# Layer totals of a graph network: one product and a VectorE transpose instead of four products and an ACT copy, at other places of the step

## What is computed

```python
z = jnp.einsum('nc,kco->nko', x, W)                       # 64 taps of 32 x 32
msg = jnp.zeros((src.shape[0], W.shape[2]), x.dtype)
for s in range(basis.shape[1]):                           # 8 corners of a cell
    msg = msg + basis[:, s, None] * z[src, wi[:, s]]
agg = jax.ops.segment_sum(msg, dst, num_segments=n)       # sum over a node's edges
agg = agg / jnp.clip(cnt, 1.0)[:, None]
return agg + x @ R + b
```

## Time and profile before

| | us |
|---|---|
| runs, median of 3 | 20890.9 (20882.26 to 20961.26) |
| profiled execution, its own time | 20959.69 |
| span of the profiled execution | 20957.9 |
| first part, until the first step of the first layer | 6021.5 |
| a layer's 98 steps | about 4790 to 4820, three times |

### The profile page before, as it was taken

One profiled execution on the slowest core, in us unless ns is written; L12 is line 12 of the kernel. 1 busy time (PEld: TensorE's weight loads), 2 busy tenths in 40 slices (PEclk: granted clock), 3 DMA queues, 4 the chain that ended last, 5 costly groups with the idle time before them and its releaser, 6 DMA issues.

```text
span 20957.9 us, 179979 instructions
## 1 busy us (share of the span) xinstructions
PE 15299.0 (73%) x55111; PEld 8212.8 (39%) x55111; DVE 11387.0 (54%) x19145; ACT 3304.1 (16%) x4009; POOL 11380.3 (54%) x12003
## 2 busy tenths in 40 slices
PE   7788888888866767676666676667666676766676
PEld 3333333333333444443433343444443343434343
DVE  4556666656655555555545555555555555555555
ACT  1111111111111111111111111111111111111111
POOL 5445555555545555555545555555554555555554
PEclk7666666666678888888878888888887888888888
DMA  1000000000010000000010000000001000000000
GB/s 33 13 14 15 15 15 15 15 14 15 15 24 16 16 16 16 16 16 16 16 23 16 17 16 16 16 16 16 17 16 23 16 16 16 16 16 16 16 16 22
DMA packets 886190, 353.06 MB, mean 17 GB/s; under 512 B 604191, under 2 KB 877680, under 8 KB 885872
## 3 DMA queue, kind: packets, MB, share of 16 engines
q0 software_dynamic: 386208, 210.78, 5.9%
q1 hardware_dynamic: 329276, 112.29, 2.3%
q10 hardware_dynamic: 170644, 29.29, 0.8%
HBM read 314.88 MB, written 36.56 MB: 17 GB/s over the span
## 4 chain that ended last, share of the span: by engine, by line
PE 51%; another core or an unknown queue 28%; issue 14%; ACT 3%; DVE 3%; ACTq 1%; DMA 0%; POOL 0%; DVEq 0%; SPq 0%; POOLq 0%
PE ps L1547 17%; PE ps L1559 16%; PE ps L1459 5%; PE ps L1570 4%; PE ps L1475 3%; ACT big L792 2%; PE ps L1448 2%; PE ps L1442 2%; DVE big L1056 1%; PE ps L1432 1%; ACT big L710 1%; ACTq L802 1%; ACT big L700 0%; PE ps L1414 0%
## 5 line engine op out<-in xcount | busy, mean ns | idle before, releaser
L571 POOL DMA_INDIRECT xg<-x_rows,idx x8790 | 8316.4, 946 | 6310.6 <-DVE big L1254 3682.7
L1547 PE MATMUL ps<-big 128*128 128x256 f32 x18816 | 5050.5, 422 | 1286.7 <-ACT big L792 1250.4
L1237 DVE TENSOR_TENSOR big<-ps,onehot 128x1024 f32<-128x1024 f32 x2352 | 2864.7, 1218 | 5084.9 <-remote 3417.8
L1547 PEld LDWEIGHTS ps<-big 128*128 128x128 f32 x18816 | 3863.2, 211 | 3111.9 <-issue 2581.3
L571 POOL DMA_INDIRECT xg<-in_x,idx x3125 | 2974.6, 952 | 2806.5 <-DVE big L1026 1826.0
L1570 PE MATMUL ps<-big,w_taps 128*32 128x512 f32 x9408 | 1544.9, 734 | 3060.8 <-issue 2851.8
L792 ACT COPY big<-ps 128x1024 f32<-128x1024 f32 x2352 | 2353.5, 1013 | 8828.4 <-PE ps L1547 5318.7
L1559 PE MATMUL ps<-xw,big 128*128 128x512 f32 x8232 | 3671.5, 597 | 50.5 <-issue 23.2
L1459 PE MATMUL ps<-w,big 65*128 65x256 f32 x6272 | 2498.1, 541 | 126.9 <-DVE big L1056 85.6
L1559 PEld LDWEIGHTS ps<-xw,big 128*128 128x128 f32 x8232 | 1543.4, 190 | 2006.9 <-issue 1981.1
L1459 PEld LDWEIGHTS ps<-w,big 65*128 65x128 f32 x6272 | 1566.0, 267 | 1875.0 <-issue 1562.7
(11 more groups left out here) (139 smaller groups left out, 6620.8 us busy)
## 6 DMA issues: line engine op xcount, KB each, us to landing
xg<-x_rows,idx POOLq DMA_INDIRECT x8790
xg<-in_x,idx POOLq DMA_INDIRECT x3125
row_of<-pick_rows SPq DMA_DIRECT2D x294, 128.0 KB
agg_rows<-rts ACTq DMA_DIRECT2D x294, 64.0 KB
meta<-in_coord_t SPq DMA_DIRECT2D x294, 48.0 KB
big<-in_rad SPq DMA_DIRECT2D x196, 64.0 KB
meta<-meta_items SPq DMA_DIRECT2D x392, 32.0 KB
idx<-in_src_t SPq DMA_DIRECT2D x392, 16.0 KB
```

Of the source, the lines that this page charges most:

```text
L571: return nc.gpsimd.indirect_dma_start(out=dst_tile, out_offset=None, in_=table, in_offset=bass.IndirectOffsetOnAxis(ap=index, axis=0))
L1237: v.tensor_tensor(bm[:, ring], hat_outer[:, its].rearrange("p n c b -> p n (c b)").unsqueeze(3) .to_broadcast([P, 4, 16, J]), onehot[:, it ...
L1547: tr = nc.tensor.matmul(ps[:, 2 * (ch % 2) + r // 2, 256 * (r % 2):256 * (r % 2) + 256], xm[:, at].rearrange("p a c -> p (a c)"), bm[:, at ...
```

## The change

Totals: one product with `fold` as the weights (32 columns) and all 512 columns of `R` moving, in place of four products with `R` as weights. It leaves 32 x 512 totals in bank 7, not turned. DVE turns them (32 x 32 blocks) straight out of PSUM into `rts` (`turn_layer`) and signals `rt_out`; ACT copies nothing any more and stores 32 rows of 2 KB instead of 512 pieces of 128 bytes. Places: the scan stands behind chunk 3 instead of 2 on DVE; the totals behind chunk 4 instead of 3 on PE; the turn behind chunk 6 on DVE; the store ahead of chunk 7 instead of 4 on ACT; tap products 0 and 1 behind chunk 6, 2 and 3 behind chunk 7, instead of one behind each of chunks 4 to 7.

```diff
-        rts = sb("rts", [P, ROW0])
+        rts = sb("rts", [2 * CH, ROW0])
             def l1_step(l, i, par, with_rows):
                 for ch in range(8):
-                    if ch == 4 and with_rows:
+                    if ch == 7 and with_rows:
                         l1_rows(l, i - 2)
             def l1_rows(l, i):
-                act.wait_ge(rt_ready, l * STEPS + i + 1)
-                act.wait_ge(rows_stored, rows0(path) + 16 * (l * STEPS + i))
-                nc.scalar.copy(rts[:, 0:P], ps[:, 7, 0:P]).then_inc(rt_out, 1)
                 act.wait_ge(rt_out, (l + 1) * STEPS + i + 1)
-                to = agg_rows[ds(i * STEP, STEP), :].rearrange("i (q s f) -> s i q f", q=4, s=4)
-                act.dma_start(to, rts[:, 0:P].rearrange("p (q f) -> p q f", q=4)).then_inc(rows_stored, 16)
+                act.dma_start(agg_rows[ds(i * STEP, STEP), :], rts[0:CH, 0:ROW]).then_inc(rows_stored, 16)
+            def turn_layer(l, i):
+
+                dve.wait_ge(rt_ready, l * STEPS + i + 1)
+                dve.wait_ge(rows_stored, rows0(path) + 16 * (l * STEPS + i))
+                v.transpose(rts[0:CH, 0:ROW], ps[0:CH, 7, :]).then_inc(rt_out, 1)
-                    if ch == 2 and with_scan:
+                    if ch == 3 and with_scan:
                         scan(n - 2, prior + LINKS1, P, l + 1, par, twice - 2)
+                    if ch == 6 and with_scan:
+                        turn_layer(l, i - 2)
                 for i in (STEPS - 2, STEPS - 1):
                     scan((l + 1) * STEPS + i, steps[0], P, l + 1, i % 2, 2 * (i // 2 + 1))
                     steps[0] += SCAN
+                    turn_layer(l, i)
             def totals_by_cell(n):
                 pe.wait_ge(R_ready, n + 1)
-                for q in range(4):
-                    tr = nc.tensor.matmul(ps[:, 7, CH * q:CH * q + CH],
-                                          R[:, 4 * q:4 * q + 4, :].rearrange("p s i -> p (s i)"), fold[:],
-                                          start=True, stop=True)
-                tr.then_inc(rt_ready, 1)
+                nc.tensor.matmul(ps[0:CH, 7, :], fold[:], R[:].rearrange("p s i -> p (s i)"), start=True, stop=True,
+                                 tile_position=(0, 0)).then_inc(rt_ready, 1)
-                    if with_totals and ch == 3:
+                    if with_totals and ch == 4:
                         totals_by_cell((l + 1) * STEPS + i - 2)
-                    if with_taps and ch >= 4:
-                        tap_products(l, i - 1, 1 - par, ch - 4)
+                    if with_taps and ch >= 6:
+                        for t in (2 * ch - 12, 2 * ch - 11):
+                            tap_products(l, i - 1, 1 - par, t)
```

More of the change, by code:

```diff
@@ L976, in turn_first @@
                     dve.wait_ge(rows_stored, 32 * n)
-                v.transpose(rts[0:2 * CH, 0:ROW], R[0:2 * CH].rearrange("p s i -> p (s i)")).then_inc(rt_out, 1)
+                v.transpose(rts[:, 0:ROW], R[0:2 * CH].rearrange("p s i -> p (s i)")).then_inc(rt_out, 1)
+            def turn_layer(l, i):
+                dve.wait_ge(rt_ready, l * STEPS + i + 1)
+                dve.wait_ge(rows_stored, rows0(path) + 16 * (l * STEPS + i))
+                v.transpose(rts[0:CH, 0:ROW], ps[0:CH, 7, :]).then_inc(rt_out, 1)
             base0 = steps[0]
```

## The result

| | before | after |
|---|---|---|
| median of the runs, us | 20906.85 (20882.26 to 20961.26, 4 runs) | 21165.83 (21105.84 to 21216.51, 4 runs) |
| span of the profiled execution, us | 20957.9 | 21146.0 |
| a step, mean of the three layers, us | 49.54 | 50.14 |

The ratio is 1.0119, with a 95% interval of 1.0084 to 1.0154: the change costs 259 us. The forecast had the direction, and 1180 us. The time lies within its stated range of 20,700 to 22,300 us, but by an order of the stretches that its sum did not have.

A forecast was written before the change was run, and what follows sets the result against it. It took GpSimd's gathers and PE's held signals as the bound. Terms of the new step summed to 53.7 us against 49.5; 285 steps x 4.15 gave +1180 us, so 22,070 us, range 20,700 to 22,300.

The forecast's parts named there:

- What bounds the kernel: Layers' steps: GpSimd's 37.5 us of gathers and the gaps between its stretches are the path, 49.5 us a step.
- The rule of the hold: PE's signals sent over about 9 us into unbroken gathers are held, the later ones until 4.07 us behind the stretch's end.
- Totals, transpose, store, scan: Changed parts: totals 1.2 us for 0.81, transpose 0.7 plus 0.1 wait, ACT's 0.27 copy gone without gain; store, scan nothing.
- Taps: PE's same 16 products, two groups later; four groups of 1.0 us each now stand behind chunks 6 and 7.
- rival 2: Stretches of 8 and 22 stay, totals' signal in time; two tap groups later cost +2.1 us a step: 21,490 us; chance .05.
- The new step: A stretch of 23 gathers, hold, then chunk 4, totals, transpose, chunk 7 and preparation in a row: 53.7 us, +4.2 a step.
- The new wait: VectorE waits for the totals' signal between chunks 6 and 7, ahead of gather group 3 and the next step's preparation.
- Rival 1: Groups 3 and 0 count as one stretch, two stretches of 15: 52.5 us a step, +3.0, 21,740 us; chance .15.
- Rival 4: No difference: VectorE doesn't wait for the totals (49.4 us a step), or the hold fits any order: 20,860 us; chance .10.
- Rival 3: Totals held only 8.5 us, 30 gathers one stretch: 19,780 us; weaker form: store packets cause the hold; .20 with other gains.
- The bound of 0.5%: About what a measurement of this kernel can tell: faster by over 0.5% .20, within .10, slower .70.

The follow-up runs named there:

- 26 gathers: Kernel before without the fourth gather of each group of a layer's step, 26 gathers in place of 30: ratio 0.9433 on chip B.
- chip E: Kernels beside the kernel before (20753 us): old PE places with turn behind 6, 0.9767; late taps with turn ahead of chunk 0, 0.9867; changed 0.9978; changed with middle pause 0.9206.
- short pause: Kernel before with GpSimd filling a row of 512 numbers ahead of each group of gathers: ratio 0.9609 on chip C, 1.0917 on chip A.
- taps early: Kernel before with the first tap group behind chunk 4 and the other three behind chunk 5: ratio 0.9937 on chip D.
- the new way at the old places: Changed kernel with totals behind chunk 3, scan, store and taps at their old places, turn ahead of the next step's chunk 0: ratio 1.0002 on chip D.
- turn at 6, old taps: Changed kernel with totals behind chunk 3, taps behind chunks 4 to 7, scan behind 2, turn still behind chunk 6: ratio 0.9767 on chip E.
- taps alone: Kernel before with only the four tap groups moved behind chunks 6 and 7, two and two: ratio 1.0359 on chip C, 0.9999 on chip A.

## Why the prediction was wrong

- **What bounds the kernel.** Right wherever signals are held: GpSimd's gathers and the held signals are the path (26 gathers, pauses). The rule of the hold was read too narrowly. "Until 4.07 us behind the last gather" is the value for 22 gathers; in after, the last held signal comes about 3.0 us behind a stretch of 15 and 4.0 to 4.5 behind 23, and with the new way of the totals chunk 4's signal no longer has to be the last (see chip E). A gap of 1 to 2 us between stretches doesn't clear it (signals are held at any age of the next stretch, with the short pause too); with a pause of 2.5 us they pass in its first 4 us. And on chip A nothing is held at all, so it was no property of the kernel alone.
- **Totals, transpose, store, scan.** Right to be small, sizes within the bounds (totals 1.05 at the full clock and 1.92 at the low one, transpose 0.704); together no time at the old places. That nothing comes back from them was wrong: they change when the held signals pass.
- **Taps.** I let them run beside the rest, and counted 2.1 us for them in rival 2. Alone they cost 2.5 us on chip C: that was a cost left out of the forecast's sum. But with the new way of the totals and the turn ahead of chunk 0 the same late taps stand in a kernel 1.3% faster than before (chip E). The taps have no fixed price either.
- **The new step, 53.7 us. This is the step that failed.** Its sum is right for the one step that I wrote down: such steps took 54.1 us. It has group 3 start 0.78 us behind chunk 7 and end 1.65 us before group 0 starts, and from that gap it takes that the stretch of 23 comes back in every step. The gap is there in the even steps (1.4 us). In the odd steps, the ones with the 23, GpSimd starts group 3 2.29 us behind chunk 7, and group 3 runs into group 0 without a gap. So a 23 never follows a 23: the next step is mostly (15, 15, 7), 50.4 us (33 times of 46), and that pair takes 52 us a step. More than half of the steps have other orders still, such as the pair (22, 8, 7) and (8, 15) at 48.7 us in after (46.5 and 46.8 on chips B and E). The mean of the mixture is 50.1 us. No run takes the 1.5 us away, so that the forecast's cycle would hold without them isn't shown; and what makes the good pairs isn't derived here.
- **The new wait "is what decides".** It is there (6.9 us ahead of each transpose), but it isn't a cost by its length. In the kernel with old taps and the turn behind 6 the wait for the totals stands at the same place, only 2.6 us long, in a step that is 1.6 us shorter than before (0.0233 x 20753 / 294).
- **Rivals.** Rival 1 had the mechanism of every second step of the bad pair: groups 3 and 0 as one stretch, the picks' signal held, chunk 3 late, a second stretch of 15 (stretches of 15 are the most frequent, 0.9 a step). It gave the reason as a pause too short to count; in fact there is no pause. It had 52.5 us for each step, where those steps take 50.4. Rival 4's second form ("the hold simply fits itself to any order") is the nearest in time. Rival 3's weaker form is out: 137,592 packets went, and the signals are held as before.
- **The bound of 0.5%.** The result lies 1.2% over the kernel before, but the same kernel gave 1.000, 1.007 and 0.998 on chips B, D and E, which hold signals. The share of the good pairs is what differs; on chip B (8, 15) with (22, 15) or (22, 8, 7) prevails. The change is no loss in general.

**What stays open.** What in the chip holds PE's signals, and why nothing was held in chip A's sitting. Why the totals' signal, and chunk 4's behind it, pass earlier with the new way of the totals: the new product has 2 passes in place of 8, and another engine waits for it; no run separates these. The chip alone is not the reason, as chip D has both behaviours (taps early, and the new way at the old places). What GpSimd does in the 1.5 us ahead of group 3 of the odd steps. The theory "the turn's place cuts the stretch" explains one kernel (turn at 6, old taps) and not the other, and isn't shown as the cause. What tips a chip towards the good or the bad pairs isn't known either.

## What to carry to other kernels

When a step is a loop of waits, follow the sum over several steps until the state, not one wait, repeats, and check the smallest gap in it on both halves of a loop that holds two steps: here a margin of 1.65 us fell to a delay of 1.5 us that stands in one half only. Where signals arrive late in long unbroken stretches of gathers, a deliberate pause of about 1.6 us after each 7 or 8 gathers can be worth more than any placing of the work (7.5% here); but measure on more than one chip, since it costs its own length where nothing is held. A part that is measured alone (+3.6%) is no term of a sum as long as the order can change.

## What the runs showed of the hardware

- One of the five chips A to E ran the kernel before in 15,375 us, the others in 20,718 to 21,022. The busy time of the layers' gathers is the same (8297 us with the taps alone on chip A, 8316 us in the kernel before): GpSimd's part of the difference is waiting.
- Only PE's signals are held: of VectorE's and ScalarE's at least nine in ten pass within 0.01 us, in the same traces.
- GpSimd starts a group's first gather some 0.8 us behind the chunk it waited for, but 2.29 us in one place of its loop, group 3 of the odd steps (138 of 138 times in after).
- Where signals are held, pauses of GpSimd make the kernel faster: by 3.9% with 1.2 us, 7.5% with 1.6 us, 4.0% with 2.5 us (there GpSimd itself is the bound again, at 47.3 us a step).
- The data of a stretch's last gather land 1.06 us behind it, whatever its length, while held signals of PE come until about 3.0 us (15 gathers) or 4.1 us (22) behind it: it isn't the gathers' transfers that they wait for.
- A fill of one partition's 512, 1024 or 2048 numbers takes GpSimd 0.51, 0.94 and 1.79 us, and a wait for it some 0.7 us on top.
